# Node pass of a four-layer graph network: the last bias moves from GpSimd to VectorE, and ScalarE, TensorE and SyncE take the slots in another order

## The reference, cut to what matters

```python
h = relu(layernorm(x));  x = x + gat(h, src, dst, edge_attr, ...)    # five GAT layers, two heads
h = relu(layernorm(x));  x = x + hgt(h, src, dst, edge_type_2, ...)
h = relu(layernorm(x));  x = x + gcn(h, src, dst, ...)               # gelu at its end
h = relu(layernorm(x));  x = x + cat(h, src, dst, edge_type_4, ...)
```

## Time and profile before

| | |
|---|---|
| median of 3 runs | 5288.45 us (5280.31 to 5296.6) |
| profiled execution | 5304.34 us |
| its span in the trace | 5302.5 us |
| busy over the span: PE, DVE, ACT, POOL | 4286.2, 4063.1, 3350.7, 3197.7 us |

### The profile page before, as it was taken

The page is one execution under the profiler, slowest core; times in us unless marked ns, Lnnn a source line. Parts: engine busy times, 40 slices in busy tenths (PEclk is TensorE's granted clock), DMA queues, the critical chain, the costliest instruction groups (busy, mean ns, idle before and its releaser), DMA issues. The chain is left out here.

```text
span 5302.5 us, 101785 instructions
## 1 busy us (share of the span) xinstructions
PE 4286.2 (81%) x28013; PEld 3711.1 (70%) x28013; DVE 4063.1 (77%) x15022; ACT 3350.7 (63%) x9065; POOL 3197.7 (60%) x2906
## 2 busy tenths in 40 slices
PE   4899999999976978969969958876895958879575
PEld 4777777788765867858858847644775847757475
DVE  5799999999985766757757767787676959859765
ACT  2778888887745766847847847643773537758400
POOL 2777777777787727737547367222761257566277
PEclk6999999999987988989989979955997979989755
DMA  3999987665535646636636546487773759857332
GB/s 93 177 222 224 222 223 224 221 216 207 197 140 120 143 86 129 140 78 139 128 91 140 113 104 145 106 248 226 167 153 88 196 141 250 234 111 132 74 94 85
DMA packets 1107279, 825.55 MB, mean 156 GB/s; under 512 B 209510, under 2 KB 1068202, under 8 KB 1106396
## 3 DMA queue, kind: packets, MB, share of 16 engines
q1 hardware_dynamic: 1026800, 690.47, 50.0%
q0 software_dynamic: 77040, 128.08, 12.4%
q10 hardware_dynamic: 2880, 0.50, 0.1%
HBM read 374.78 MB, written 448.11 MB: 155 GB/s over the span
## 5 line engine op out<-in xcount | busy, mean ns | idle before, releaser
L807 POOL DMA_INDIRECT gat_G<-table,k_src_row x980 | 1077.6, 1100 | 318.8 <-issue 284.6
L1600 ACT ACTIVATE gat_Gw<-gat_G,gat_al 128x128 f32<-128x128 f32 x1960 | 618.5, 394 | 88.8 <-DVE gat_al L1425 88.8
L1456 DVE SCALAR_TENSOR_TENSOR gat_Gw<-gat_own,gat_al,gat_Gw 128x128 f32<-128x128 f32 x1960 | 554.4, 342 | 69.2 <-ACT gat_Gw L1600 69.0
L1717 PE MATMUL gat_psG<-gat_ends_at,gat_Gw 128*128 128x128 f32 x3920 | 539.6, 282 | 42.6 <-DVE gat_Gw L1456 42.5
L1745 PE MATMUL gat_psZ<-gat_aggT,t_gat_wh 128*128 128x256 f32 x1960 | 526.4, 392 | 15.1 <-ACT gat_hT L1626 14.7
L1717 PEld LDWEIGHTS gat_psG<-gat_ends_at,gat_Gw 128*128 128x128 f32 x3920 | 495.1, 198 | 53.6 <-DVE gat_Gw L1456 50.5
L636 PEld LDWEIGHTS nodes_psR<-t_ident_v,nodes_hTl 128*128 128x128 f32 x3168 | 432.5, 192 | 106.0 <-issue 1.8
L481 POOL TENSOR_TENSOR nodes_rstd<-nodes_var,k_half 128x14 f32<-128x14 f32 x141 | 368.4, 2613 | 185.4 <-DVE nodes_var L546 182.7
L636 PE MATMUL nodes_psR<-t_ident_v,nodes_hTl 128*128 128x132 f32 x3168 | 447.2, 278 | 0.0
L1626 ACT ACTIVATE gat_hT<-gat_psZ,t_gat_bias 128x256 f32<-128x256 f32 x490 | 231.2, 472 | 268.1 <-PE gat_psZ L1746 265.4
L1745 PEld LDWEIGHTS gat_psZ<-gat_aggT,t_gat_wh 128*128 128x128 f32 x1960 | 339.5, 193 | 56.4 <-ACT gat_aggT L1607 17.0
(11 more groups left out here) (667 smaller groups left out, 12659.0 us busy)
## 6 DMA issues: line engine op xcount, KB each, us to landing
table<-nodes_rows SPq DMA_DIRECT2D x660, 198.0 KB
table<-nodes_n SPq DMA_DIRECT2D x396, 192.0 KB
gat_own<-table SPq DMA_DIRECT2D x490, 132.0 KB
table<-gat_rows SPq DMA_DIRECT2D x392, 132.0 KB
nodes_x<-in_x SPq DMA_DIRECT2D x132, 192.0 KB
out<-nodes_x_out SPq DMA_DIRECT2D x132, 192.0 KB
gat_G<-table,k_src_row POOLq DMA_INDIRECT x980
hgt_q<-enter_q SPq DMA_DIRECT2D x98, 144.0 KB
```

Of the source, the lines that this page charges most:

```text
L807: eng.indirect_dma_start(to, None, table, bass.IndirectOffsetOnAxis(ap=index, axis=0)).then_inc(sem, 16)
L1456: ins = eng.scalar_tensor_tensor(Gw[:, i % RS, t, h, :], own[:, i % RO, t, 0:D], al[:, g % 2, 1, a:a + 1], Gw[:, i % RS, t, h, :], ALU.mul ...
L1600: ins = eng.activation(Gw[:, i % RS, t, h, :], G[:, i % RG, t, 0:D], ACT.Copy, scale=al[:, g % 2, 0, a:a + 1])
L1717: mm = eng.matmul(o[:, h * P:(h + 1) * P], Gw[:, i % RS, t, h, :], ends_at[:, i % RE, t, :], start=True, stop=True)
```

## The change

Four edits, all in `node_pass`:

1. The add of the last bias (`xb`) leaves POOL and is done by DVE in the same round, behind the statistics of the next block and slots.
2. On ACT, gelu of block k-7 stands ahead of the copies of the scores; it stood behind the norm of block k.
3. On ACT, the norm of the slots (`nS`) goes to behind `hTs`, near the end of the round.
4. PE turns the slots of group k-1 (not k) in round k, `hTs` is of that group too, and the scores, their copies and the store of `srows` are of group k-2 (not k-1).

The amount of work and of data is the same. The diff, cut to its core:

```diff
 # SP
-                    if is_slots(k - 1):
-                        m = slot_tiles(k - 1)
-                        eng.wait_ge(s.nS, k)
-                        eng.wait_ge(s.scoresS_out, k)
-                        eng.dma_start(slots_view(K.tables[0], K.rows, k - 1), srows[:, (k - 1) % RB, 0:m, :]
-                                      ).then_inc(sts[(k - 1) % RB], 16)
+                    if is_slots(k - 2):
+                        m = slot_tiles(k - 2)
+                        eng.wait_ge(s.nS, k - 1)
+                        eng.wait_ge(s.scoresS_out, k - 1)
+                        eng.dma_start(slots_view(K.tables[0], K.rows, k - 2), srows[:, (k - 2) % RB, 0:m, :]
+                                      ).then_inc(sts[(k - 2) % RB], 16)
...
 # POOL
-                def with_bias(b):
-                    if b == 0:
-                        eng.wait_ge(s.bias, 2)
-                    eng.wait_ge(x_in[b % XB], 16 * (b // XB + 1))
-                    if b >= XB:
-                        eng.wait_ge(s.x1, b - XB + 1)
-                    eng.tensor_tensor(xb[:, b % XB, :, :], x[:, b % XB, :, :], spread(last_b[:, :], 1, T), ALU.add).then_inc(s.xb, 1)
...
-                    if is_block(k):
-                        with_bias(k)
...
 # DVE
                     if is_slots(k + 1):
                         n_stats += stats_of_slots(k + 1)
+                    if is_block(k):
+                        if k >= XB:
+                            eng.wait_ge(s.x1, k - XB + 1)
+                        eng.tensor_tensor(xb[:, k % XB, :, :], x[:, k % XB, :, :], spread(last_b[:, :], 1, T), ALU.add).then_inc(s.xb, 1)
...
 # PE
-                        eng.wait_ge(s.hTs, min(a + 1, NS))
+                        eng.wait_ge(s.hTs, min(a, NS))
...
-                    if is_slots(a):
-                        for t in range(slot_tiles(a)):
+                    if is_slots(b):
+                        for t in range(slot_tiles(b)):
...
-                    if is_slots(k):
-                        eng.wait_ge(s.nS, k + 1)
+                    if is_slots(a):
+                        eng.wait_ge(s.nS, a + 1)
                         eng.wait_ge(s.hT0, k + 1)
-                        turn(psA, lambda t: srows[:, k % RB, t, 0:D], slot_tiles(k)).then_inc(s.turnedS, 1)
+                        turn(psA, lambda t: srows[:, a % RB, t, 0:D], slot_tiles(a)).then_inc(s.turnedS, 1)
```

More of the change, by code:

```diff
@@ L535, in _ @@
                 eng.wait_ge(s.bias_in, 32)
+                eng.wait_ge(s.bias, 2)
                 for k in range(LAST + 1):
@@ L745, in _ @@
                         rows_out(3, b)
+                    c = k - 7
+                    if is_block(c):
+                        eng.wait_ge(s.z6, c + 1)
+                        if c >= 2:
+                            eng.wait_ge(s.x3, c - 1)
+                        eng.activation(g6[:, c % 2, :, :], z6[:, c % 2, :, :], ACT.Gelu).then_inc(s.gelu, 1)
                     if is_block(a):
                         eng.wait_ge(s.scored0, a + 1)
-                        eng.wait_ge(s.scoredS, min(a + 1, NS))
+                        eng.wait_ge(s.scoredS, min(a, NS))
                         eng.activation(rows0[:, a % RB, :, D:ROWW], psA[:, W:W + 4 * T].rearrange("p (t c) -> p t c", c=4),
                                        ACT.Copy).then_inc(s.scores0_out, 1)
-                    if is_slots(a):
-                        m = slot_tiles(a)
+                    if is_slots(b):
+                        m = slot_tiles(b)
                         got = psA[:, at_score:at_score + 4 * m].rearrange("p (t c) -> p t c", c=4)
-                        eng.activation(srows[:, a % RB, 0:m, D:ROWW], got, ACT.Copy)
-                        eng.activation(K.sc[:, :, SC * a:SC * (a + 1), :].rearrange("p j t h -> p t j h"),
+                        eng.activation(srows[:, b % RB, 0:m, D:ROWW], got, ACT.Copy)
+                        eng.activation(K.sc[:, :, SC * b:SC * (b + 1), :].rearrange("p j t h -> p t j h"),
                                        got.rearrange("p t (j h) -> p t j h", j=2), ACT.Copy
@@ L766, in _ @@
                         ins.then_inc(s.nA, 1)
[L767 to L772, removed]
                     c = k - 6
@@ L776, in _ @@
                         eng.activation(hT6[:, :], psB[:, 0:W], ACT.Relu).then_inc(s.hT6, 1)
[L777 to L784, removed]
                     if is_block(b):
@@ L793, in _ @@
                         eng.activation(hT7[:, :], psC[:, 0:W], ACT.Relu).then_inc(s.hT7, 1)
+                    if is_slots(a):
+                        w = slot_tiles(a) * P
+                        eng.wait_ge(s.turnedS, a + 1)
+                        eng.activation(hTs[:, 0:w], psA[:, 0:w], ACT.Relu).then_inc(s.hTs, 1)
                     if is_slots(k):
-                        w = slot_tiles(k) * P
-                        eng.wait_ge(s.turnedS, k + 1)
-                        eng.activation(hTs[:, 0:w], psA[:, 0:w], ACT.Relu).then_inc(s.hTs, 1)
+                        if k >= RB:
+                            eng.wait_ge(sts[k % RB], 16 * (k // RB))
+                        for t in range(SC):
+                            ins = eng.activation(srows[:, k % RB, t, 0:D], xg[:, k % SG, t, :], ACT.Relu,
+                                                 bias=shift[:, k % 4, at_s + t:at_s + t + 1],
+                                                 scale=rstd[:, k % 4, at_s + t:at_s + t + 1])
+                        ins.then_inc(s.nS, 1)
                     c = k - 4
```

## The result

| | before | after |
|---|---|---|
| median | 5291.02 us (5280.31 to 5296.6, 4 runs) | 5167.95 us (5161.38 to 5171.49, 4 runs) |
| profiled execution, span | 5304.34, 5302.5 us | 5161.38, 5159.7 us |
| ratio of the medians, 95% interval | | 0.9768 [0.9749, 0.9788] |

The change wins 123 us, 2.3%. The forecast was 5200 with a range from 5172 to 5245. The direction came out, and both halves of the change act as described, but the gain is larger than the 110 us to which the upper bounds of the terms add up.

What follows compares the result with a forecast made beforehand. PE's wait behind ACT was taken to bound slot rounds, DVE's collisions with POOL's add the rest; 57 + 28 + 3.6, together 88 us, off 5288.45 gave 5200 us, range 5172 to 5245.

Steps and rivals of the forecast that it cites:

- upper bounds of the terms: Node pass: largest gains for slot rounds, tail and 9 early rounds, 73 x 0.95 + 34 x 0.98 + 9 x 0.8 = 110 us.
- The add on DVE: Node pass, DVE: new add about 546 ns, collisions with POOL's add gone, DVE's need with slots 10.35 to about 9.64 us.
- The wait of PE: Slot rounds: PE's stop behind ACT, 0.69 to 0.95 us a round, goes; 0.78 taken, 73 rounds, 57 us.
- Gelu "costs nothing": ACT, node pass: gelu's 0.52 us fills the 0.57 us wait for the scores, so moving it costs nothing.
- The tail: Rounds without slots at the node pass's end: 10.10 to 9.28 us each, 34 x 0.82 = 28 us won.
- The start-up at nothing: Node pass before 300 us, with gathers and half-filled rounds: no gain counted.
- DMA as the bound: Slot rounds: queues carry no more than 222 GB/s, rounds stay 10.81, only the tail's 28 us won: 5260; chance 0.10.
- The add held by the power: DVE's new add waits until POOL's power ends, 1.25 us without slots, 0.45 with; about 50 us won: 5238; chance 0.07.
- The ring: Late stores from the three `srows` buffers hold ACT before the slots' norm; slower, 5336; chance 0.05.
- No gain: PE's wait only moves, to L710 behind `hT7` or L655 behind the late relu: about 5280; chance 0.05.

Runs made afterwards that it cites:

- The idle add: The changed kernel, with POOL also doing its old add at the old place into a buffer nobody reads: 5302.81 us, ratio 1.0016.
- second profiles: The kernels before and after, unchanged, profiled once more: before 5305.35 us, after 5170.83 us, ratio 0.9774.
- experiment 2: The kernel before with only the add moved to DVE, the order of ACT, PE and SP as before: 5260.64 us, ratio 0.9944.
- experiments 2 and 5: For experiment 2 see its line; the other is the changed kernel with gelu back behind the norm of block k: 5198.29 us, ratio 0.9836.
- Experiment 4: The changed kernel with the add on POOL, just ahead of its power, where DVE's adds read PSUM: 5192.5 us, ratio 0.9823.
- experiments 7 and 9: Changed kernel with two `srows` buffers, not three: 5352.84 us; changed kernel with turns reordered on PE, `hT7` and `hTs` moved on ACT: 5152.57 us.

## Why the prediction was right or wrong

**The add on DVE: right.** It costs 542 ns where 546 was expected, the collisions are gone, and DVE's need came out at 9.65 (98.97% of 9.75) where 9.64 was given. The idle add shows that the collision, not the dependence, was DVE's cost.

**The wait of PE: right in place, too small in size.** This is the step that failed: "PE's own need, 10.81 less 0.69 to 0.95, is 9.86 to 10.12", and in the sum 73 x 0.78 = 57 us. Measured are 9.75 us a round in after, and for the 73 rounds 80 us (78 by the second profiles). By the starts, a round before took 10.85; the 10.81 came from a count of rounds. In the second profile of before the same three steps are these:

```profile
801.15 0.94 PE L701 MATMUL nodes_psB<-k_gcn_w,nodes_hT 128*128 128x128 f32 x6
...
802.78 0.41 PE L628 MATMUL nodes_psA<-k_ident,nodes_srows 128*128 128x128 f32 x2 [0.69 <-ACT nodes_hT L789]
...
803.06 0.94 PE L710 MATMUL nodes_psC<-k_cat_out,nodes_hT 128*128 128x128 f32 x6
...
803.84 0.49 PE L646 MATMUL nodes_psY<-nodes_hT,first_gat_wm 128*128 128x384 f32 x1
```

1.63, 0.28 and 0.78 us, against 0.67, 0.22 and 0.70 after: 0.96, 0.06 and 0.08 won, 1.10 in all, and 1.10 is what a round became shorter. On average over the slot rounds the steps are 1.62, 0.29 and 0.77 before and 0.67, 0.22 and 0.71 after. The prediction's upper bound, 0.95, was about the first step alone, and it took 0.78, below the middle of its own bounds (0.82) and below PEld's wait (0.85). The time between the starts was the right reading; the recorded waits were too short. The other 0.14 lie in the two groups behind the stop: the turn's 0.29 I took as undisturbed from a row that itself stood behind the stop, and the last product I did not count. Gelu put back tests this by itself: 0.15 recorded, 0.36 lost. That the weight loads lose their lead is what the rows show with it; that it is the reason is argued, not shown.

**Gelu "costs nothing": right, but it gave something, which the prediction put at nothing.** It fills ACT's wait for the scores. But I saw it only as making way for `hT0`; its move also brings `hT6` in time for the GCN product, whose load waited 0.15 to 0.16 us before. With gelu put back 30 us are lost, and the tail's rounds are 0.22 longer.

**The tail: right in number, in part by luck.** 28 us forecast, 28 measured; 9.32 a round against 9.28. But the prediction gave PE's need without slots as 10.10 - 0.74 = 9.36 or a little less, with nothing for ACT's order; experiment 2 has the add without that order, and its tail is at 9.56, 20 us won. The other 0.24 come from the order on ACT, which the prediction counted for slot rounds only: with gelu put back the tail is at 9.54, with the slots' norm put back at 9.37. In rounds without slots the last product's load waits for `hT7` about 0.40 us with gelu at its old place (experiments 2 and 5), 0.18 in after. PE sets the tail now, and still waits that little (1100 to 1380 us):

```profile
PEld nodes_psC L705 <- ACT nodes_hT L780: 5.3, 30, 0.2
```

**The start-up at nothing: wrong.** Of the first 25 rounds I counted 9, at half the gain, 3.6 us; they gave 16 to 26. I had no row for them and wrote "nothing" where I should have written a bound. By the second profiles the sum is 16 + 78 + 28 = 122 us, beside the 123 of the medians; that pair of profiles differs by 132, and the other 10 us lie behind the node pass, as in the first pair.

**The rivals.** *DMA as the bound* fell: the core moved 248 GB/s at 700 us, where it had moved 222, and from 300 to 400 us 240 at the share of 1.04 at which before moved 234. *The add held by the power* fell: the new add takes 535 to 587 ns in all 132 rounds of after, and in 110 of them it lies within the power. One of these:

```profile
759.10 2.62 POOL L473 TENSOR_TENSOR nodes_rstd<-nodes_var,k_half 128x14 f32<-128x14 f32 x1 [0.73 <-DVE nodes_var L537]
...
760.94 0.54 DVE L559 TENSOR_TENSOR nodes_xb<-nodes_x,nodes_last_b 128x384 f32<-128x384 f32 x1
```

The Trainium skill, "SBUF — State Buffer", section "SBUF: two separate sides", limits the lock on DVE's side to operations with two SBUF inputs or in a two-port mode. With that part experiment 4 agrees (551 and 552 ns with PSUM, 694 without); with a lock for the whole of the power these rows do not. *The ring* fell, with the small margin that experiments 7 and 9 show. *No gain* fell.

## What to carry to other kernels

Read the cost of a stop on an in-order engine from the start of one instruction to the start of the next, over the groups behind the stop too, against the same groups in free flow; the recorded wait was less than the cost in all three stops here (0.69 and 1.10, 0.15 and 0.36, 0.46 and 0.71 us). Where two engines are both near the round's length, price the need of each without its own disturbance: here removing one alone won 33 or 29 us, and removing both 123. A number that comes out does not show that its terms were right: the tail's 28 us came from two causes, of which one was counted. A POOL operation that nobody waits for can still set the time, through the DVE operations that it falls on.

## What was not expected of the hardware

A full busy share of PE does not mean that it runs at its rate: 499.76 of 500 us busy at 10.11 us a round, and 100.00 of 100 at 9.75 and at 9.64, for the same matmuls and at a granted clock of 1.00 in all three stretches. And one POOL add of 1.0 us costs a DVE operation of 128x14 that it meets about 1.5 us (0.18 to 1.71), more than it costs an add of 27 times the size (0.54 to 1.79).
